# Transformer block on one Trainium2 core: loads issued by SP, and a new order at both ends of the attention

## What is computed

```
x = x + layernorm(attention(layernorm(x)))          # x: 16 batches x 512 tokens x 128 channels
x = x + layernorm(moe(layernorm(x)))

attention: q, k, v = x@W + b, 16 heads of 8; rotary embedding on q and k;
           causal softmax(q k^T / sqrt(8)) v; @ Wp + bp
moe:       scores = softmax(x @ gate_w + gate_b); the two best of 16 experts per token, weighted by score
           y = sum of  silu(x@w1 + b1) * (x@w3 + b3) @ w2 + b2   over those two
           z = silu(x@sw1 + sb1) * (x@sw3 + sb3) @ sw2 + sb2      (shared expert, inner width 352)
           moe = y + z
```

## Time and profile before

| | us |
|---|---|
| median of 3 runs | 1196.63 (1194.95 to 1196.68) |
| the profiled execution | 1198.38 |
| its span | 1195.8 |
| PE busy in the span | 1055.4 (88%) |
| POOL busy | 847.6 (71%) |
| DVE busy | 846.7 (71%) |
| ACT busy | 739.4 (62%) |

### The profile page before, as it was taken

One profiled execution on the slowest core, in us unless ns is written; L12 is line 12 of the kernel. 1 busy time (PEld: TensorE's weight loads), 2 busy tenths in 40 slices (PEclk: granted clock), 3 DMA queues, 4 the chain that ended last, 5 costly groups with the idle time before them and its releaser, 6 DMA issues.

```text
span 1195.8 us, 26783 instructions
## 1 busy us (share of the span) xinstructions
PE 1055.4 (88%) x8456; PEld 689.4 (58%) x8456; DVE 846.7 (71%) x2285; ACT 739.4 (62%) x1617; POOL 847.6 (71%) x984
## 2 busy tenths in 40 slices
PE   1389999999999999999999999999768999999700
PEld 1255565665656656566565665655445888888600
DVE  4288888787787877878778777775233666666586
ACT  0117777676776767767777777778523555555434
POOL 5536668788787887878878776667763666666567
PEclk9659999999999999999999999999968999999955
DMA  5333332314323143231432324224122444444275
GB/s 93 103 93 112 96 105 78 113 58 135 114 69 113 58 138 108 72 113 59 137 111 68 104 62 136 77 67 133 45 77 76 124 126 141 144 126 126 91 238 179
DMA packets 104854, 126.13 MB, mean 105 GB/s; under 512 B 17613, under 2 KB 85518, under 8 KB 100110
## 3 DMA queue, kind: packets, MB, share of 16 engines
q1 hardware_dynamic: 91638, 104.54, 29.8%
q0 software_dynamic: 8704, 18.11, 4.3%
q10 hardware_dynamic: 4376, 1.80, 0.6%
HBM read 78.06 MB, written 45.42 MB: 103 GB/s over the span
## 4 chain that ended last, share of the span: by engine, by line
PE 84%; DVE 7%; POOL 2%; issue 2%; DMA 2%; ACT 1%; ACTq 1%; SPq 0%; POOLq 0%; DVEq 0%
PE heads_ps L1472 13%; PE score L1462 12%; PE wide L1500 12%; PE wide L1622 7%; PE wide L1438 7%; PE wide L1502 5%; PE score L1450 3%; PE wide L1533 3%; PE wide L1603 3%; PE wide L1604 3%; PE score L1594 3%; PE misc L1480 2%; PE wide L1620 2%; DVE f_st L1082 1%; DVE mx L1279 1%
## 5 line engine op out<-in xcount | busy, mean ns | idle before, releaser
L943 ACT ACTIVATE values<-score 128x512 f32<-128x512 f32 (+1 forms) x704 | 371.4, 558 | 121.9 <-PE score L1462 111.8
L1279 DVE TENSOR_REDUCE mx<-wide 128x2 f32<-128x1024 f32 (+3 forms) x384 | 393.2, 1043 | 74.1 <-PE wide L1502 69.7
L1500 PE MATMUL wide<-qk 72*128 72x512 bf16 (+3 forms) x1024 | 247.7, 306 | 7.1 <-DMA qk<-parts_scratch 3.2
L834 POOL TENSOR_SCALAR_AFFINE_SELECT values<-values 128x512 f32<-128x512 f32 x256 | 174.4, 690 | 107.0 <-ACT values L943 105.7
L1462 PE MATMUL score<-qk 75*128 75x512 bf16 (+3 forms) x1024 | 229.1, 300 | 1.6 <-ACT values L943 0.9
L879 POOL DMA_INDIRECT token_scratch<-spread,e_id x144 | 137.9, 958 | 95.5 <-issue 74.2
L1502 PE MATMUL wide<-maskneg,identb 128*128 128x128 bf16 x1024 | 199.2, 223 | 0.0
L1472 PE MATMUL heads_ps<-values 128*32 128x512 f32 (+3 forms) x2048 | 174.1, 441 | 0.0
L823 POOL DMA_INDIRECT sorted_scratch<-zr,places x128 | 127.4, 995 | 31.4 <-issue 28.2
L1500 PEld LDWEIGHTS wide<-qk 72*128 72x128 bf16 x1024 | 101.6, 99 | 78.0 <-issue 18.7
L1462 PEld LDWEIGHTS score<-qk 75*128 75x128 bf16 x1024 | 87.3, 98 | 97.0 <-ACT values L943 46.3
(11 more groups left out here) (194 smaller groups left out, 1961.8 us busy)
## 6 DMA issues: line engine op xcount, KB each, us to landing
qk<-parts_scratch SPq DMA_DIRECT2D x192, 192.0 KB
parts_scratch<-spread SPq DMA_DIRECT2D x16, 768.0 KB
qk<-sorted_scratch SPq DMA_DIRECT2D x144, 66.0 KB
front<-token_scratch SPq DMA_DIRECT2D x16, 512.0 KB, 3.8
xt<-attn_x SPq DMA_DIRECT2D x16, 256.0 KB, 8.4
xr<-attn_x SPq DMA_DIRECT2D x16, 256.0 KB, 8.7
x_scratch<-z SPq DMA_DIRECT2D x16, 256.0 KB, 6.4
shared_scratch<-s_out SPq DMA_DIRECT2D x16, 256.0 KB, 8.4
```

The costliest lines, as they stand in the source:

```text
L834: nc.gpsimd.affine_select(out=prob[n][:, :, 0:P], in_=prob[n][:, :, 0:P], compare_op=ALU.is_ge, fill=0.0, base=0, pattern=[[0, HG], [1, P] ...
L943: nc.scalar.activation(free_ap(prob[kb][:, hs_[0], :], [[1, N * len(hs_)]]), score[SCORE_RING.buffer(b, step)][:, 0:N * len(hs_)], ACT.Exp ...
L1279: nc.vector.tensor_reduce(mx[:, h0:h0 + len(hs_), j:j + 1], src, axis=AX.X, op=ALU.max).then_inc(p1_max, 1)
L1500: nc.tensor.matmul(o, q4[e][0:ROWS, h, j * P:(j + 1) * P], k4[e][0:ROWS, h, 0:L], start=True, stop=False)
```

## The change

It does five things.

1. The 15 loads and the 1056 KB store move from ACT's queue to SP's, behind the ten weight loads and ahead of SP's main loop. The three bias_rows DMAs move from ACT (step splits) to SP, in pass i = -3, behind batch 1's input load and ahead of the store of batch 0's parts.
2. START is a new list.
3. DRAIN is a new list.
4. Twelve filling matmuls are put at the head of PE's queue.
5. Before the experts there were two runs of 8 filling matmuls, one before and one after the wait for the first blocks; now there is one run of 6 before it.

```
-FILL = 8
+FILL = 6
+FIRST_FILL = 12
...
 START = (
-    "rstd@1 stats@1 X@1 normal@1 stats@2 Q@1 cos@1 splits@1 fold@1 rstd@2 X@2 normal@2 sin0@1 sin1@1 sin2@1 Q@2 "
...
+    "rstd@1 X@1 stats@1 Q@1 normal@1 cos@1 sin0@1 stats@2 V sin1@1 T@1 sin2@1 splits@1 second@1 sin3@1 X@2 fold@1 "
...
 DRAIN = (
...
-    "d0@-1 d1@-1 d2@-1 rX choose rL chosen rexp U0@-1 G0@-1 D H1@-1 K@-1 counts@-1 place@-1 blocks@-1 ends@-1 "
...
+    "rL rexp U0@-1 chosen G0@-1 H0@-1 K@-1 counts@-1 place@-1 D blocks@-1 ends@-1 rows@-1 d0@-1 d1@-1 d2@-1 U1@-1 "
...
 # SP
             sp.dma_start(cos_sb[:], cos).then_inc(weights_in, 16)
             sp.dma_start(sin_sb[:], sin).then_inc(weights_in, 16)
+            sp.dma_start(bias_f[:, 0:INTER], b1).then_inc(bias_in, 16)
+            sp.dma_start(bias_f[:, INTER:], b3).then_inc(bias_in, 16)
+            for w, s in ((sw1_sb[:], sw1), (sw3_sb[:], sw3),
...
+                sp.dma_start(w, s).then_inc(f_fw, 16)
+            for c, (at, m) in enumerate(CH):
+                sp.dma_start(sb3_col[0:m, c:c + 1], sb3[at:at + m].rearrange("(h o) -> h o", o=1)).then_inc(f_fw, 16)
+                sp.dma_start(sb1_col[0:m, c:c + 1], sb1[at:at + m].rearrange("(h o) -> h o", o=1)).then_inc(f_fw, 16)
+            sp.wait_ge(ident_ready, N_IDENT)
+            sp.dma_start(sorted_d[E * CAP:, :].rearrange("(n p) c -> p n c", p=P),
+                          free_ap(blank[:], [[1, SPARE], [1, ROW]], SPARE)).then_inc(spare_filled, 16)
...
                     sp.dma_start(xt[:], x_v[i + 4]).then_inc(x_in, 16)
+                if i == -3:
+                    sp.wait_ge(bias_split, 1)
+                    sp.wait_ge(rows_cleared, 3)
+                    for r in range(NPART):
+                        sp.dma_start(bias_rows[r * E:(r + 1) * E, :], bias_parts[:, r, :]).then_inc(bias_kept, 16)
...
 # PE
             pe.wait_ge(ident_ready, N_IDENT)
             pe.wait_ge(filled, 4)
+            kept_busy(FIRST_FILL)
...
-                if isinstance(n, int) and n == 0:
-                    kept_busy(FILL)
```

More of the change, by code:

```diff
@@ L590, in _ @@
             sp.dma_start(sin_sb[:], sin).then_inc(weights_in, 16)
+            sp.dma_start(bias_f[:, 0:INTER], b1).then_inc(bias_in, 16)
+            sp.dma_start(bias_f[:, INTER:], b3).then_inc(bias_in, 16)
+            for w, s in ((sw1_sb[:], sw1), (sw3_sb[:], sw3),
+                         (sw2_sb[:, 0:NCH - 1, :], sw2[0:(NCH - 1) * P, :].rearrange("(c h) d -> h c d", h=P)),
+                         (sw2_sb[0:sb2_at, NCH - 1, :], sw2[CH[-1][0]:, :]), (sw2_sb[sb2_at:sb2_at + 1, NCH - 1, :], row(sb2)),
+                         (gw_sb[:], gate_w), (gb_bc[:], row(gate_b).to_broadcast([P, E]))):
+                sp.dma_start(w, s).then_inc(f_fw, 16)
[5 more added lines that the diff above has]
+                          free_ap(blank[:], [[1, SPARE], [1, ROW]], SPARE)).then_inc(spare_filled, 16)
             def maxima_in(b, e, half):
@@ L907, in _ @@
                 act.dma_start(k4[n][ROWS:SROWS, :, :], free_ap(onesb[0:NPART, :], [[0, NH * NT], [1, P]])).then_inc(rows_filled, 16)
[L908 to L919, removed]
             def body(i):
@@ L930, in body @@
                         unit = wide[WIDE_RING.buffer(b, step)]
[L931 to L936, removed]
+                    if step.what == "s":
                         kb, hs_ = P2_UNITS[n]
@@ L1386, in _, with kept_busy @@
             pe.wait_ge(filled, 4)
+            def kept_busy(count):
+                for _ in range(count):
+                    nc.tensor.matmul(heads_ps[:], onesb[:], free_ap(onesb[:], [[0, NT], [1, P]]), start=True, stop=True)
+            kept_busy(FIRST_FILL)
             def body(i):
@@ L1573, in experts_of @@
                 return list(values)
-            def kept_busy(count):
-                for _ in range(count):
-                    nc.tensor.matmul(heads_ps[:], onesb[:], free_ap(onesb[:], [[0, NT], [1, P]]), start=True, stop=True)
             def x_across(n, k, r, j):
```

## The result

The changed kernel takes 1185.55 us (median of 5 runs, 1184.49 to 1188.33); the kernel before, run 5 times beside it, 1196.68 (1194.95 to 1198.56). The ratio is 0.9906, with a 95% interval of 0.9890 to 0.9921. That is faster by over 0.2%, and inside the range of 1177 to 1190, but 3.95 us above the forecast of 1181.6. The profiled execution took 1186.67 us (before 1198.38), its span is 1184.1 (before 1195.8).

A forecast was written before the change was run, and what follows sets the result against it. TensorE was taken as busy without a break from about 100 to 870 us, so gains lie at both ends: 1198.38 - 8.8 - 6.2 = 1183.4 profiled, less the 1.75 offset 1181.6 us for the median; range 1177 to 1190.

The forecast's parts named there:

- Start: First 90 us: a chain with four waits, to be shortened so the second pass starts 8.8 us earlier.
- p0: Scores of the first pass, after the parts' store and 14.73 us of transfers; forecast at 48.65 instead of 58.71.
- second pass: Batch 0's first second-pass score, forecast at 79.9 instead of 88.75, after a 31.3 us stretch from p0.
- The bias rows ahead of the store: On SP, waiting for DVE's split; delay the parts' store from 31.85 to 33.9, giving back 2.05 us.
- First fill: Twelve filling matmuls before X wake TensorE's array: Q 1.62 us shorter, X about 0.5 earlier, together 2.1 us.
- End: Passage from attention to experts: scatters 2.1, second fill 3.4, full-clock experts 0.7, together 6.2 us; 4.5 otherwise.
- The earlier last scatter: Batch 15's scatters on POOL fill its idle time before H1 and H2; last ends at 897.55, 2.1 us saved.
- Middle chain: Rival at the start: batch 1's POOL path or batch 2's X comes too late; 1184.6 to 1186.6, chance 0.12.
- Single queue: Rival: batch 1's input lands late behind the 1056 KB store on SP's queue; 1186.6 to 1189.6, chance 0.10.
- Slower: Rival: SP's DMA issues held 3.94 us each; seven to ten give 1202 to 1212, all fifteen 1229.5; chance 0.04.
- Gate: Rival at the start: the filling matmuls don't wake the array; total 1183.7, chance 0.06.
- no effect: Rival: no change in total, only possible if both ends hide something unseen; chance 0.02.

The follow-up runs named there:

- e6: Changed kernel with the three bias_rows DMAs behind batch 0's shuffles instead of ahead of the store; 1229.23 us on the slower second chip, ratio 0.9892 to before.
- e11: Changed kernel run once more without any edit, in another set; 1184.77 us, ratio 0.9894 to before.
- e3: Changed kernel without the twelve filling matmuls at the start; 1187.34 us, ratio 0.9910 to before.
- e12: Changed kernel with bias rows behind shuffles, four scatters ahead of H0, no fill before the experts, and two filling matmuls between U0 and K; 1181.78 us, ratio 0.9874.
- e5: Kernel before with only one run of 6 filling matmuls ahead of the wait for the first blocks; 1237.94 us on the slower second chip, ratio 0.9973.
- e1: Kernel before with the new DRAIN list alone, old fills and old start; 1194.55 us, ratio 0.9971 to before.
- e2: Changed kernel with the old DRAIN and the old two filling runs of 8, so the front alone; 1188.05 us, ratio 0.9921 to before.
- e9: Kernel before with the new START list alone, loads and bias rows staying on ACT; 1197.22 us, ratio 0.9998 to before.
- e4: Changed kernel with two filling matmuls (a bridge) between batch 15's U0 and K; 1184.94 us, ratio 0.9879 to before.
- e10: Changed kernel with bias rows behind shuffles, four scatters ahead of H0, H2 behind the last, no fill before the experts; 1183.03 us, ratio 0.9881 to before.
- e7: Changed kernel with D of batch 14 back ahead of H0 and K; 1226.38 us on the slower second chip, ratio 0.9888 to before.
- e8: Changed kernel with the old START list, keeping the moved loads, first fill and new end; 1238.78 us on the slower second chip, ratio 0.9984.

## Why the prediction was right, and where it was not

**Start: right in size and step.** Q at 13.7 was forecast and 14.00 came; T 24.1 and 23.92; parts ready 31.85 and 31.88; p0 48.65 and 47.58; second pass 79.9 and 79.62, -9.13 us for a forecast of -8.8. Two of its terms were off and nearly cancel, so the closeness at the second pass is in part luck. The bias rows ahead of the store cost 1.1 (e6), not 2.05: DVE's split took 2.8 us (28.09 to 30.87), not the 3.59 taken from before. And the clock was forecast to come up before Q of batch 2 ends, -0.7; Q took 3.49 at half speed. Without that term the sum is 30.04 + 1.94 = 31.98, and 32.04 came; but e11, the same kernel, has 31.76, and the same START takes 30.68 in e3, so this stretch can't confirm a term of 0.7. The prediction called TensorE the limit of the stretch. That holds only at half clock: from 59 to 62 us of the changed kernel, at a clock of 1.00, TensorE is busy 1.78 of 3 us and DVE 2.78, so an earlier return of the clock may win less than TensorE's rows say. Q's start hangs on two things at once: the weights (sin took 7.8 us to land) and ACT's copy; in e12 sin took 8.9 and Q started at 14.82.

**First fill: right.** 2.1 us at T (e3). The clock line of the profile's page would have said otherwise: it reads 1.00 in e3 from 14 to 18 us, where Q runs at half speed.

**End: right in mechanism; part of it hangs on the clock.** The second filling run cost what was forecast (3.4; e5 3.48). The earlier last scatter (2.1) came as 2.19 in e1 and 1.92 in e11, but as 0.29 in the first profile, since D at half clock (+1.5) holds H0 and all scatters behind it. My first theory for that, K's place ahead of D with the short pause before it, fell with e1 and e11 (same order, 2.96) and e2 (old order, 4.05). What decides when the clock returns after U0 stays open: U0 takes 3.58 to 3.76 us for four matmuls in every profile but e9's (3.35), before's too, near half speed (batch 15's U1 and U2, eight matmuls, take 3.70 in e11), and the return falls now ahead of D, now inside it. e4's bridge can't be told from chance with one profile. The experts' start at full clock was forecast at 0.7. The last stretch is 0.45 us shorter, but e2, whose experts start at half clock (first transpose 0.42 us), takes 286.71 us from x_across to the end, as long as the changed kernel, so even the 0.45 isn't shown to come from the clock. In e11, from the last scatter to x_across passed 5.96 us, where 0.4 less was forecast (5.57 from the earlier trace rows). I took it over unchanged, and it didn't stay.

**The middle: not in the forecast.** The stretch from the second pass to U0 was taken as unchanged; it grew by 1.16 and 1.07 us in the two profiles of the changed kernel. It goes with the clock: the stretch is 786.92 before, 786.69 in e1 (874.01 - 87.32) and 786.51 in e10 (864.17 - 77.66), none with a dip, and 789.54 in e4 (869.15 - 79.61), with a deep one. On the second chip it is 801.85 in e6, with a dip, and 798.36 to 799.10 in the other three, without. Of the kernels with both the new front and the new end, e3, e7, e10 and e12 have no dip, and the changed kernel, e11, e4 and e6 do. No run tells what sets it off. Transfers at full load (DMA share 1.16) are there before too (1.13), without a dip.

**The median: a small miss of its own.** The forecast took off 1.75 us, because before's profiled execution stood that much above the median of three runs. The changed kernel's median is 1.12 under its profiled execution. So the miss of 3.95 us is 3.3 from the terms above (15.0 forecast, 11.7 measured in the span) and 0.6 from this offset. By e11, whose profiled run is its median, the terms missed 1.4 us (13.6 of 15.0). The offset itself is poorly known: beside the changed kernel before's median was 1196.68 over five runs, but beside e1 to e4 and e9 to e12 it was 1198.32 and 1198.20, over 13 and 15 runs, which is the profiled 1198.38. That may be the chips or few runs; no run tells.

**The rivals.** Middle chain: X of batch 2 ended 2.0 us ahead of p0, close to the slack counted, and nothing was lost. Single queue: the input landed at 23.1 us for a forecast of 21.5, right behind the 1056 KB store (issued 16.42, landed 6.5 us later). Its issue came at 16.97, 3.1 later than the 13.9 forecast, because SP was held; from there it took 6.1 us and not 7.6 (before, beside the store on ACT's queue, 4.1). The Trainium skill, "DMA: Bandwidth & Descriptors", Queues, rings and completion order, says that a ring is consumed in order; this landing agrees. It was in time for the new list, while with the old one (e8) it cost all of the front's gain. Slower: SP was held, 2.37 us on sin, 0.95 and 1.10 on the two biases and 1.77 on batch 1's input, where the usual issue takes 0.43; seven holds of 3.94 were needed. Gate and no effect: excluded by e3 and by the total.

## What to carry to other kernels

Moving work off an engine's queue and reordering the list of steps may each be worth nothing and together 9 us: look at what stands in each queue between the freed instruction and the one that waits, and test the halves apart. A wait of several sources has the next one close behind: four scatters ahead of H0 won 2.85 us at the scatters and 0.78 at the experts, because SP's queue, with the tail stores in it, was then the later one. And take the offset between a profiled run and the median from more than three runs, or leave it out, when the forecast is about 1%.

## What the hardware showed that was not expected

- The granted clock of the page reads 0.9 in the first slice, yet X takes 1.08 us and Q 3.57 where they take 0.84 and 1.97 behind the fill. In e3, without the fill, the window from 14 to 18 us reads 1.00. At the start of these programs the durations tell the array's speed, and the column doesn't.
- The same kernel, twice: D of batch 14 takes 4.52 us in one profile and 2.92 in the other, with the same instructions ahead of it. A single profile can't carry a verdict of 1.5 us there.
- Late in the last regular iteration the granted clock fell to 0.50 although TensorE was busy: in the changed kernel it is busy for the whole of 822.75 to 826.75 us, at 0.70. Four of the fourteen profiles have this dip, and all fourteen have the same ORDER. What sets it off stays open.
- Issuing is not of constant length: SP's sin took 2.37 us to issue here and 0.52 before, with the same ten issues ahead of it on SP. Before, it was a load on ACT, issued right behind, that was held for 3.94 us.
